# Layer norms batch by batch on GpSimd, and the second attention's queries turned and projected one step earlier

## The reference

```python
def _layernorm(x, axis=-1, eps=1e-05):
    m = jnp.mean(x, axis=axis, keepdims=True)
    v = jnp.var(x, axis=axis, keepdims=True)
    return (x - m) / jnp.sqrt(v + eps)
...
    def _L0_xattn_ref(queries, keys, values, mask, Wq, bq, Wk, bk, Wv, bv, Wo, bo):
        ...
        q = split_heads(queries @ Wq + bq)
        k = split_heads(keys @ Wk + bk)
        v = split_heads(values @ Wv + bv)
        scores = jnp.einsum('bhqd,bhkd->bhqk', q, k) / jnp.sqrt(jnp.float32(HD))
        scores = jnp.where(mask, jnp.float32(-1000000000000000.0), scores)
        attn = jax.nn.softmax(scores, axis=-1)
        ctx = jnp.einsum('bhqk,bhkd->bhqd', attn, v)
        ctx = ctx.transpose(0, 2, 1, 3).reshape(b, sq, d)
        return ctx @ Wo + bo
...
    x = x + _L0_attn_ref(_layernorm(x, axis=-1), ...)
    x = x + _L0_xattn_ref(_layernorm(x, axis=-1), ctx_1024, ctx_1024, mask_Bx1xSxS2_bk1, ...)
    x = x + _L0_ffn_ref(_layernorm(x, axis=-1), ...)
```

## Time and profile before

| | us |
|---|---|
| three runs | 332.83, 333.5, 335.4 (median 333.5) |
| the profiled execution | 333.79 |
| its span, first to last instruction | 332.0 |
| PE busy | 299.7 (90%) |
| DVE busy | 282.9 (85%) |
| ACT busy | 220.6 (66%) |
| POOL busy | 173.9 (52%) |

### The profile page before, as it was taken

How to read it: one execution, slowest core, us unless ns; L and a number is a source line. 1 busy time by engine, 2 the same in 40 slices (tenths; PEclk the granted TensorE clock), 3 DMA queues, 4 the chain that set the end, 5 groups by cost and what they waited for, 6 DMA issues and landing times.

```text
span 332.0 us, 6308 instructions
## 1 busy us (share of the span) xinstructions
PE 299.7 (90%) x1704; PEld 205.1 (62%) x1704; DVE 282.9 (85%) x575; ACT 220.6 (66%) x456; POOL 173.9 (52%) x249
## 2 busy tenths in 40 slices
PE   0899958999999999999979979688999999999995
PEld 0634745666655656555655757556777777777773
DVE  3997885788987887987894879999999999999994
ACT  1296726967885668467553987656787677777773
POOL 9440020000170069116138778477888789888883
PEclk9999995999999999999999999999999999999999
DMA  7700031031120311110003766556664766667721
GB/s 286 241 1 0 2 63 24 11 63 34 37 61 2 64 35 33 34 33 2 2 0 92 220 181 197 163 162 199 190 209 136 226 223 186 224 208 227 218 88 63
DMA packets 30892, 36.84 MB, mean 111 GB/s; under 512 B 5136, under 2 KB 22288, under 8 KB 30736
## 3 DMA queue, kind: packets, MB, share of 16 engines
q1 hardware_dynamic: 30864, 36.51, 37.1%
HBM read 31.77 MB, written 0.79 MB: 98 GB/s over the span
## 4 chain that ended last, share of the span: by engine, by line
PE 45%; DVE 17%; issue 13%; POOL 11%; SPq 7%; DMA 4%; ACT 3%; DVEq 0%; POOLq 0%; ACTq 0%
PE bank L382 33%; POOL qbd L1463 6%; SPq L358 5%; POOL kst L1440 3%; DVE conv L1358 2%; PE bank L504 2%; PE bank L529 2%; DMA conv<-coefficient_rows 2%; DVE kst L1149 2%; SPq L347 2%; DVE rawmax L1112 2%; DMA xres<-x 1%; PE bank L757 1%; DVE qbd L1128 1%; PE bank L759 1%
## 5 line engine op out<-in xcount | busy, mean ns | idle before, releaser
L382 PE MATMUL bank<-khl,kst 128*128 128x512 f32 x396 | 106.1, 403 | 10.3 <-DVE kst L1149 8.2
L1463 POOL TENSOR_TENSOR qbd<-vs,qbd 128x512 fp32r<-128x512 f32 x65 | 84.4, 1299 | 29.2 <-ACT qbd L992 29.0
L382 PEld LDWEIGHTS bank<-khl,kst 128*128 128x128 f32 x396 | 70.1, 188 | 38.4 <-DVE kst L1149 19.3
L962 ACT ACTIVATE bank<-bank 128x512 f32<-128x512 f32 x62 | 36.1, 582 | 33.4 <-PE bank L382 33.3
L1112 DVE TENSOR_REDUCE rawmax<-bank 128x4 f32<-128x512 f32 x64 | 43.0, 683 | 13.7 <-PE bank L382 12.8
L1149 DVE TENSOR_TENSOR kst<-ring,kst 128x256 fp32r<-128x256 f32 x62 | 49.2, 794 | 0.0
L992 ACT ACTIVATE qbd<-vs 128x512 fp32r<-128x512 f32 x66 | 41.2, 624 | 9.5 <-DVE vs L1367 4.9
L1367 DVE TENSOR_TENSOR vs<-conv,bank 128x512 f32<-128x512 f32 x62 | 42.6, 687 | 3.2
L1358 DVE TENSOR_TENSOR conv<-bank,conv 128x512 f32<-128x512 f32 x61 | 41.6, 682 | 4.3 <-DMA conv<-coefficient_rows 2.0
L255 POOL TENSOR_SCALAR nwt<-mv 128x4 f32<-128x4 f32 x4 | 0.9, 228 | 75.6 <-DVE mv L1007 75.6
L1440 POOL TENSOR_TENSOR kst<-ring,kst 128x128 fp32r<-128x128 f32 x64 | 38.9, 608 | 0.3
(11 more groups left out here) (190 smaller groups left out, 506.9 us busy)
## 6 DMA issues: line engine op xcount, KB each, us to landing
conv<-coefficient_rows SPq DMA_DIRECT2D x122, 128.0 KB, 3.0
ring<-w SPq DMA_DIRECT2D x66, 192.0 KB, 2.9
kbd<-kst SPq DMA_DIRECT2D x60, 64.0 KB, 2.0
pa<-pack_a SPq DMA_DIRECT2D x1, 1140.0 KB, 6.5
xres<-x SPq DMA_DIRECT2D x1, 512.0 KB, 4.2
ctxs<-ctxT SPq DMA_DIRECT2D x1, 512.0 KB, 7.1
outT<-qc SPq DMA_DIRECT2D x2, 256.0 KB, 2.0
pb<-pack_b SPq DMA_DIRECT2D x1, 449.0 KB, 7.9
```

What stands on the lines that cost most here:

```text
L382: return pe.matmul(out, lhsT, rhs, start=start, stop=stop)
L962: act.activation(out, four(2 + p), ACT.Silu).then_inc(silu_done, 1)
L1463: pool.tensor_tensor(hlo[:, k % 4, :].rearrange("p (b t) -> p b t", b=4), hx[k % 4], hhi[:, k % 4, :].bitcast(F32).rearrange("p (b t) -> p ...
```

## The change

It has three parts.

1. The norms on GpSimd. `normalise_all` is the old code for the prologue's norm on VectorE. The new `normalise(eng, link, n, b)` takes one batch: three operations, then two for each Newton step, each with the running value as a per-row scalar, on one column, and one scaling. GpSimd calls it for each batch of n = 1, and for n = 2 for batches 0 to 3 between the expert weights it prepares, and for 4 to 7 after its share of the experts' inputs (`low_inputs(0)`).
2. `turn_inputs` of steps 6, 10 and 14 moves from the end of the step to ahead of its first transposed scores, and `second_queries` from the head of the `making` step into the `inputs` step. ScalarE's copies move along: `copy_inputs` ahead of the first exponential, `expert_inputs` ahead of the third, and the rounding of the queries behind the fourth.
3. In the `making` step the first stack stands right behind `turn_max`, the others between the products; the odd ones, in bank 5, wait for `qbd` as well. VectorE takes the low part ahead of its casts to `qbd`, and the last stack's copy comes after `norm`.

```diff
-            for c in range(2):
-                normalise(pool, link, 1, 4 * c, 4 * c + 4, False)
-                add_bias(pool, Bw("bo"), 4 * c, 4 * c + 4, B + 4 * c + 4)
+            for b in range(B):
+                normalise(pool, link, 1, b)
+                if b % 4 == 3:
+                    add_bias(pool, Bw("bo"), b - 3, b + 1, B + b + 1)
...
+        def normalise(eng, link, n, b):
+
+            v, y, a, vh = (nwt[:, i, b:b + 1] for i in range(4))
+            eng.wait_ge(stats_ready, B * n + b + 1)
+            link(eng.tensor_scalar(v, mv[:, b, 1:2], EPS, None, ALU.add))
+            link(eng.tensor_scalar(vh, v, -0.5, None, ALU.mult))
+            link(eng.tensor_scalar(y.bitcast(I32), v.bitcast(I32), -0.5, RSQRT_MAGIC, ALU.mult, ALU.add))
+            for at, to in ((y, v), (v, y), (y, v)):
+                link(eng.tensor_scalar(a, at, at, vh, ALU.mult, ALU.mult))
+                link(eng.tensor_scalar(to, a, 1.5, at, ALU.add, ALU.mult))
+            eng.wait_ge(xT_done, 2 * n - 1 + b // 4)
+            eng.tensor_scalar(xn[:, b, :], xres[:, b, :], mv[:, b, 0:1], v,
+                              ALU.subtract, ALU.mult).then_inc(xn_ready, 1)
...
+                normalise(pool, link, 2, k)
             low_inputs(0)
-            normalise(pool, link, 2, 4, B, False)
+            for b in range(4, B):
+                normalise(pool, link, 2, b)
```

On TensorE the step is afterwards written so (`making` is 0 in step 7 and 1 in step 11, `inputs` 0 in step 6 and 1 in step 10):

```diff
+                if making is not None:
+                    second_stack(making, 0)
                 if early:
                     scores(s + 1, 1)
                 later(s, 0)
-                if making is not None:
-                    second_queries(making)
...
                 if inputs is not None:
                     second_inputs(inputs)
                 if s == STEPS - 2:
                     turn_inputs(2, 0, bank[7])
+                if now:
+                    scoresT(s, 0)
+                if making is not None:
+                    second_stack(making, 1)
+                    scores(s + 1, 0)
+                if now:
+                    scoresT(s, 1)
+                if making is not None:
+                    second_stack(making, 2)
+                    scores(s + 1, 1)
+                if early:
+                    scores(s + 1, 3)
+                if s >= 1:
+                    turn_out(s - 1)
+                later(s, 2)
+                if inputs is not None:
+                    second_queries(inputs)
+                if now:
+                    scoresT(s, 2)
+                if making is not None:
+                    second_stack(making, 3)
+                    scores(s + 1, 2)
+                if now:
+                    scoresT(s, 3)
+                if making is not None:
+                    scores(s + 1, 3)
+                later(s, 3)
```

88 lines of the change are left out of this document (28 added, 60 removed).

## The result

The changed kernel takes 337.62 us (median of 20 runs, 335.39 to 341.81), the kernel before, run beside it, 336.14 (20 runs, 332.64 to 337.96). The ratio is 1.0059, with a 95% interval of 1.003 to 1.0088: the changed kernel is slower by 0.6%, some 2.0 us by the ratio and 1.5 us between the medians. The prediction was 333.8 with a range of 330.8 to 337.0, so the measured time lies above the range. Of the 3.8 us between 333.8 and 337.62 the larger part, 2.6, is the level of the comparison: the kernel before came out at 336.14 here, and at 333.5 in the three runs that the prediction had. The ratio doesn't depend on that, and it is larger than the +0.35 us of my sum. Its profiled execution took 337.40 us with a span of 335.6 (before: 333.79 and 332.0), 3.6 us more.

The account below looks back on a forecast made before the run. The prediction took attention to be bound by TensorE's queue. Its terms, 0 + 0.65 - 0.1 + 0.25 - 0.7 + 0.25 = +0.35 us, gave 333.8 us against the 333.5 median, with a range of 330.8 to 337.0.

Parts of the forecast that it names:

- part 4: Router inputs turned earlier in step 14: the router products' wait at the head of step 15 goes, -0.7 us.
- +0.25 us: Router: GpSimd's subtraction starts sooner, beside VectorE's coefficients, and slows that operation from 0.42 to 0.69 us.
- the lock: Rival: GpSimd's norms hold VectorE up in the router through exclusive SBUF access, 3 us, giving 336.8; chance 0.08.
- Part 1, the norms: GpSimd's batch-by-batch norms: 3.6 us a batch, transposes of step 6 not waiting, about 0.3 us won in step 10.
- Part 2, the projection: Turning and projecting queries a step earlier: step 6 unchanged, step 10 +0.65 us, being 0.96 less 0.3 from the norms.
- Part 3, the first stack: First stack ahead of the values: TensorE waits 2.0 and 1.8 us; step 7 -0.1 us, step 11 +0.25.
- B: Rival theory from the experiments, no chance given: GpSimd's 84 added small operations slow VectorE or lower the clock everywhere.
- The norms came in time: Rival that they don't: the two-scalar operations cost over 0.44 us, up to +3.2 us, 337.0; chance 0.05.
- Part 3's wait was not absorbed: Rival that the wait before the first stack is absorbed and steps 7 and 11 shrink, giving 332.0; chance 0.20.
- The freed GpSimd: Rival: GpSimd bounds the head of the experts and is freed 4.2 us sooner, giving 329.6; chance 0.05.
- fall of the clock: Rival: the new waits in steps 7 and 11 lower the clock, 3.4 us a time, 337.2 or 340.6; chance 0.07.

Follow-up runs that it names:

- e1: The changed kernel with one wait more: GpSimd's subtraction of step 14 starts only after VectorE has split the last maxima; ratio 1.0057 to the kernel before.
- e6: e3 without its wait for GpSimd's subtraction; steps 14 and 15 took 7.26 and 8.13 us, 15.39 together against 14.37 in e3.
- e3: The kernel before with batch-by-batch norms, step 14's router inputs turned and copied earlier, and GpSimd's subtraction held until the last split; ratio 1.0014.
- e2: The kernel before with only GpSimd's norms made batch by batch; ratio 0.9982 to the kernel before, the six steps 0.32 us shorter.
- e4: The changed kernel with the first stack behind the products with the values, ScalarE's copies reordered to match; steps 7 and 11 0.28 and 0.09 us shorter.
- e10: e8 plus early second inputs, projection last in steps 6 and 10, rounding and low part before the casts; this last grew steps 7, 11 by 0.67, 0.44 us.
- e7: e2 with the second queries turned and projected a step earlier, rounding, low part and stacks unmoved; steps 6, 7, 10, 11 together 33.23 us against 32.52.
- e8: e3 with the four transposes of the router's inputs behind step 14's last score product; ratio 0.9992 to the kernel before, six steps 0.92 us shorter.
- e5: The changed kernel with GpSimd's 512-column subtraction cut into four of 128 columns; step 14 took 6.53 us instead of 7.24.
- e11: e10 with the first stack ahead of the first transposed scores and its copy ahead of ScalarE's first exponential; steps 7 and 11 took 9.78 and 10.41 us.

## Why the prediction was wrong

The step that failed is in **part 4**, which put step 14 at nothing. There I priced a subtraction of GpSimd's in the expert units at +0.25 us beside VectorE's coefficients, at 173.9, and gave GpSimd's subtraction on the expert inputs no place at all. That one waits for ScalarE's rounding of the expert inputs alone, since GpSimd is idle by then (4.48 us). When the rounding is moved ahead of the third exponential, the subtraction moves with it. My time for the end of the copies was right: 156.15, and 5.88 us after the matmul that opens step 14 in the changed kernel, which is 156.16 on the same scale. In the kernel before the split ended at 156.04, ahead of that. But the transposes, now ahead of the last score product, which I took to cost nothing, delay the last maxima and the split by 0.47 us, onto the subtraction, and L524 waits for the split. I had followed the moved copies to TensorE and VectorE, and not to the third engine that they release. This cost 0.86 us of step 14 (e1; 0.87 by e6 against e3), 0.96 to 1.02 with step 15, the larger part of the distance between the +0.10 that I had for the six steps and the measured +1.61. The price itself stood in my text: a cast held for 0.68 us beside GpSimd's bias addition, and the lock as a rival. I had looked for the lock behind the attention only.

That the measured time lies above the range has a second reason, which no term of the sum covers: I took the three runs' 333.5 for the kernel's level, and it came out at 336.14. On a level of 333.5 the ratio would make 335.5 (an estimate), inside the range, with the step just as wrong.

Point by point:

- **Part 1, the norms.** The small operations were undersized. I took 0.31 us from one start to the next; nine take from 90.97 to 94.36, 0.38 each, since the form with two per-row scalars takes 0.34 to 0.38 us instead of 0.23. A batch takes 4.2 us, not 3.6. Of the margin of 1.1 us 0.6 was left (95.18 to 95.80), and the transposes don't wait. The gain in steps 6 and 7 (0.20 and 0.23 by e2) I had not reckoned; the 0.25 in step 10 I had, as 0.3, but not that step 11 gives it back.
- **Part 2, the projection.** +0.65 for step 10 came out at +0.66, by the terms that I named (norms -0.25, projection +0.90). The 0 for step 6 came out at -0.08, with some luck: it is the norms' -0.20 and the projection's +0.12.
- **Part 3, the first stack.** The wait is there, 1.72 and 1.50 us against my 2.0 and 1.8, and the steps came out 0.23 and 0.13 us longer than I said. It was the right mechanism but not the whole: with the wait taken away (e4) about half of its price stayed, and VectorE's low part ahead of its casts holds the first transposed scores by itself (e10). As a sum over steps 6, 7, 10 and 11, part 3 costs 0.68 us: 33.91 in e1 against 33.23 in e7.
- **Part 4, the head of step 15.** The router products no longer wait, and that is worth 0.64 us (e3, e8), against my 0.7. In step 14 the transposes ahead of the last score product cost 0.2 more, which I had set at nothing. The +0.25 in the router did not come: the coefficient operation at 177.15 took its 0.42 us, and GpSimd's subtraction of the expert units came only at 178.23, behind its last norm.

By these runs the six steps add up so: norms -0.32, early projection +0.72 (e7 less e2), rounding, first stack and stack order +0.68, router's head -0.64 with +0.21 for the early transposes, and the meeting of the two subtractions +0.96 in steps 14 and 15 (changed less e1). That is 1.61, the measured sum; being differences from kernel to kernel, they had to come near it.

**The rivals.** The lock was the right rival at the wrong place: I had it hold VectorE in the router by 3 us. In the changed kernel's router VectorE's operations on 256 columns keep their 0.41 to 0.45 us and GpSimd's stretch (the scaling of batch 7, at 177.28, takes 0.98 instead of 0.82). B fell with e2 but for 0.13 us in step 11. The norms came in time. Part 3's wait was not absorbed: steps 7 and 11 grew. The freed GpSimd shortened nothing: from the first expert product to the end it is +0.55. The new waits of part 3 brought no fall of the clock: it stood at 1.00 in each of the seven stretches shown.

**Not explained by the change** are the prologue and the expert units of the profiled execution. Up to 44 us the two kernels' prologues read alike, but the granted clock falls to 1.2 GHz at 44 in the one and not in the other. Stretches of 2 us, before:

```profile
42.00:44.00 2.00, 2.00 (x17) 1.90 (x18) 1.78 (x4) 0.79 (x3) 0.00 (x0) 1.00 0.49 98
44.00:46.00 2.00, 1.60 (x13) 1.16 (x11) 1.82 (x6) 1.16 (x2) 0.00 (x0) 1.00 0.00 0
```

The changed kernel, with two stretches of 4 us in the expert units:

```profile
42.00:44.00 2.00, 2.00 (x17) 1.90 (x17) 1.59 (x4) 0.78 (x3) 0.00 (x0) 0.98 0.51 104
44.00:46.00 2.00, 2.00 (x11) 2.00 (x11) 1.51 (x6) 1.35 (x2) 0.00 (x0) 0.50 0.02 4
46.00:48.00 2.00, 1.55 (x6) 0.86 (x5) 1.05 (x2) 0.00 (x0) 0.00 (x0) 0.67 0.00 0
...
212.00:216.00 4.00, 2.82 (x9) 2.25 (x10) 3.93 (x8) 2.44 (x6) 2.02 (x3) 0.82 0.46 129
216.00:220.00 4.00, 4.00 (x15) 3.25 (x14) 3.62 (x7) 2.84 (x6) 2.35 (x3) 0.75 0.57 167
```

The first L524 stood at 50.1 to 50.3 us in nine of the fourteen profiled kernels, the one before among them, and at 51.6 to 53.6 in the five others, the norms alone and the best by its steps (e8) among those. A fall near 212 came in six: the changed kernel, e2, e5, e6, e10 and e11. Five of them have 167.5 to 168.1 us from the first expert product to the end, e10 has 166.85, and the others have 166.6 to 167.1. The norms alone (e2) show the late L524 and the fall, while e3 and e7, which contain the norms too, show neither, so the norms do not decide it, nor do the router's pieces or the early projection; the kernel before has one profiled execution only, but the mean granted clock of its executions goes from 0.969 to 0.995 too.

Among the executions whose mean granted clock was 0.988 or more, the changed kernel took 335.39 to 335.45 us (3 of 20) and the kernel before, in the series of e1 to e4, 332.95 to 334.26, median 333.77 (12 of 35). That is a difference of 1.65 us where the steps say 1.61. In the same way e3 (3 executions) lies 0.86 us under the kernel before where its steps say 0.82, e4 (one) 1.27 above where they say 1.28, e2 (three) 0.04 above where they say 0.32 under, and e1 (two) 0.15 above where they say 0.65; so whole times at one clock bear the steps out to about half a microsecond. Whether the changed kernel falls into the lower clocks more often, 20 runs don't tell; why the clock falls in one execution and not in the next stayed open.

## What to carry to other kernels

When a step is moved ahead, follow not only who waits for it but who is released by it: an idle third engine starts at once, and what it starts may lie on an operation of 0.2 us that the critical path runs through. A short operation at the end of a chain wants its own guard (a wait, or a long neighbour cut in pieces) more than a long one does. And work taken off TensorE's queue is worth what the next engine's chain lets through: of 0.96 us moved out of each of steps 7 and 11, at most 0.4 came back (e7, step 11), while step 10, which took one of them in, paid 0.9.
